# Row maxima of two attention streams transposed and sent in two halves, and a new rule for the order of each engine's work

## The reference, cut to what matters

```python
x = x + tanh(g_xattn[0]) * L0_xattn(layernorm(x), ctx)   # 8 heads of 64, keys from ctx
x = x + tanh(g_ffn[0])   * L0_ffn(layernorm(x))          # 16 heads of 8, self-attention, plus top-2 of 8 experts
x = x + tanh(g_xattn[1]) * L1_xattn(layernorm(x), ctx)   # 16 heads of 8, keys from ctx
x = x + tanh(g_ffn[1])   * L1_ffn(layernorm(x))          # top-2 of 8 experts
```

## Time and profile before

| | |
|---|---|
| Median of 3 runs | 752.5 us (751.01 to 752.66) |
| Profiled execution | 746.59 us |
| Its span, first to last instruction | 744.8 us |
| Mean granted clock of PE in it | 0.933 of full speed |
| Busy in the span | PE 663.1, DVE 569.7, ACT 374.2, POOL 344.5 us |

### The profile page before, as it was taken

One profiled execution on the slowest core, in us unless ns is written; L12 is line 12 of the kernel. 1 busy time (PEld: TensorE's weight loads), 2 busy tenths in 40 slices (PEclk: granted clock), 3 DMA queues, 4 the chain that ended last, 5 costly groups with the idle time before them and its releaser, 6 DMA issues.

```text
span 744.8 us, 13302 instructions
## 1 busy us (share of the span) xinstructions
PE 663.1 (89%) x5232; PEld 336.2 (45%) x5232; DVE 569.7 (76%) x1055; ACT 374.2 (50%) x482; POOL 344.5 (46%) x467
## 2 busy tenths in 40 slices
PE   6699898998999899989999999989999789787684
PEld 2265454553544455434645355534653424333342
DVE  2626578589998879788898979887888987928534
ACT  4064345545546753775357644765357346263360
POOL 4273753852463257415663368326764324422233
PEclk9599999999999999989999999999999969969597
DMA  7210202112101221121121311121013221021000
GB/s 193 80 58 19 86 1 62 45 44 63 43 24 41 77 64 52 52 79 32 41 66 42 99 48 65 36 75 50 22 58 97 71 68 68 4 89 55 7 1 14
DMA packets 45790, 40.82 MB, mean 55 GB/s; under 512 B 4824, under 2 KB 37536, under 8 KB 45728
## 3 DMA queue, kind: packets, MB, share of 16 engines
q1 hardware_dynamic: 45168, 39.52, 17.1%
q10 hardware_dynamic: 560, 0.46, 0.2%
HBM read 22.93 MB, written 17.04 MB: 54 GB/s over the span
## 4 chain that ended last, share of the span: by engine, by line
PE 66%; DVE 21%; ACT 6%; issue 2%; POOL 2%; DMA 2%; SPq 1%; POOLq 0%; DVEq 0%
PE psum L670 13%; PE psum L626 7%; PE psum L590 7%; DVE mx8B L925 7%; PE psum L582 6%; DVE mxA L831 4%; PE psum L658 4%; ACT probB L740 4%; PE psum L557 3%; PE psum L639 3%; PE psum L551 3%; PE psum L600 2%; PE psum L577 2%; DVE rden L839 2%; PE psum L675 2%
## 5 line engine op out<-in xcount | busy, mean ns | idle before, releaser
L925 DVE TENSOR_REDUCE mx8B<-psum 128x2 f32<-128x1024 f32 x128 | 153.7, 1219 | 22.7 <-PE psum L639 21.5
L740 ACT ACTIVATE probB<-psum 128x1024 f32<-128x1024 f32 x128 | 126.4, 1029 | 57.2 <-PE psum L658 56.5
L727 ACT ACTIVATE probX<-psum 128x1024 f32<-128x1024 f32 x64 | 65.5, 1024 | 95.1 <-PE psum L582 94.8
L920 DVE TENSOR_REDUCE mx8F<-psum 128x4 f32<-128x1024 f32 x64 | 77.0, 1217 | 8.8 <-PE psum L633 8.6
L831 DVE TENSOR_REDUCE mxA<-psum 128x2 f32<-128x1024 f32 x64 | 76.6, 1216 | 8.5 <-PE psum L564 8.1
L839 DVE RECIPROCAL rden<-psum 128x256 f32<-128x256 f32 x32 | 56.1, 1752 | 34.8 <-PE psum L594 34.7
L740 ACT ACTIVATE probF<-psum 128x1024 f32<-128x1024 f32 x64 | 65.1, 1026 | 24.0 <-PE psum L658 22.2
L999 POOL TENSOR_TENSOR prodC<-prodC 128x256 f32<-128x256 f32 x30 | 21.8, 725 | 104.6 <-DVE prodC L913 102.3
L670 PE MATMUL psum<-probB,v8B 128*32 128x256 f32 x1024 | 67.5, 408 | 2.8 <-ACT probB L740 2.7
L582 PE MATMUL psum<-qX,kX 64*128 64x256 f32 x512 | 68.4, 388 | 0.0
L991 POOL TENSOR_TENSOR psum_k<-probX 128x512 f32<-128x512 f32 x32 | 40.8, 1274 | 59.5 <-ACT probX L727 58.5
(11 more groups left out here) (192 smaller groups left out, 1174.2 us busy)
## 6 DMA issues: line engine op xcount, KB each, us to landing
k8B<-k_dK SPq DMA_DIRECT2D x32, 192.0 KB
k_dK<-partsK SPq DMA_DIRECT2D x8, 384.0 KB, 2.5
q8F<-q_dF SPq DMA_DIRECT2D x32, 96.0 KB
k8F<-k_dF SPq DMA_DIRECT2D x32, 96.0 KB
q8B<-q_dB SPq DMA_DIRECT2D x32, 96.0 KB
k_dK<-partsK SPq DMA_DIRECT2D x8, 256.0 KB, 2.7
cTX<-in_ctxT SPq DMA_DIRECT2D x8, 192.0 KB, 2.8
cTK<-in_ctxT SPq DMA_DIRECT2D x8, 192.0 KB, 2.4
```

The costliest lines, as they stand in the source:

```text
L727: nc.scalar.activation(prob[s][(8 * b + k) % SLOTS[s]][:], ps, ACT.Exp, scale=float(XD) ** -0.5).then_inc(done["ACT"], 1)
L740: nc.scalar.activation(prob[s][(units * b + k) % SLOTS[s]][:], ps, ACT.Exp, scale=float(D8) ** -0.5).then_inc(done["ACT"], 1)
L920: nc.vector.tensor_reduce(mx8[s][:].rearrange("p t (i q) -> p i t q", i=2)[:, :, :, k], ps.rearrange("p (i t n) -> p i t n", i=2, t=QT), A ...
L925: nc.vector.tensor_reduce(mx8[s][:, t, :].rearrange("p (i q) -> p i q", i=2)[:, :, p], ps.rearrange("p (i n) -> p i n", i=2), AX.X, ALU.ma ...
```

## The change

The maxima of F and B are transposed, sent and read back in two halves of four pairs each. `mT8`, `mw` and `mr` now exist with k = 0 and 1: half 0 needs only the first half of `mx8`, and the first half of `e8` needs only half 0's `mr`. For this the maxima are laid out by half in `mx8`, `m2` becomes 8 rows by 2 halves, and `mw` and `mr` have a semaphore for each half. Each transposition works on 8 columns in place of 16; the two DVE instructions behind it keep their length of 256.

The order changes too. To the longest way of each step an amount is added for its stream and name (`URGENT`) and one for its stream and batch (`TURN`). On PE and DVE the steps whose start lies within 0.05 or 0.1 us of that engine's earliest start now count as equal (`NEAR`), and the greatest sum goes first. `LEAD`, which bounds how far ahead PE may fill for DVE, goes from 2.0 to 1.6, and some planned costs are altered. Every engine's list may come out anew.

The diff, with context lines left out:

```diff
 
-HOP, OUT, LEAD = .07, .18, 2.0
+HOP, OUT, LEAD = .07, .18, 1.6
+
+URGENT = {
+    "X": {"ctx": -1109, "e": -172, "kp": -398, "ln": 216, "ls": 1008, "mT": 1342, "mx": 477, "out": -814, "pv": -153, "qp": 137, "rs": -55, "vp": -490, "xb": -1195, "xh": 530, "xin": 252},
+    "F": {"e8": 21, "fin": -2102, "gate": -183, "gx": 487, "ln": 743, "ls": 1151, "mT8": 231, "moe": -64, "mr": 1131, "mw": -1069, "mx8": 193, "oT": 771, "pv8": -105, "qk": 73, "rs": -745, "sp": -59, "sr": -1648, "sw": 169, "v8": -231, "wT": -347, "wb": 325, "xh": 938},
+    "K": {"ctx": -327, "kk": -1014, "sp": 1076, "sr": -13, "sw": 100, "vv": 455},
+    "B": {"aT": 645, "e8": 1380, "ln": -212, "ls": 322, "mT8": 1441, "mr": -676, "mw": 1051, "mx8": -199, "oT": 200, "out8": 632, "pv8": -884, "qk": 870, "rs": 1173, "sp": 1101, "sr": 1115, "sw": 2256, "xb": 131, "xh": -395},
+    "C": {"fin": -355, "gate": 829, "gx": -964, "ln": 95, "ls": 209, "moe": -468, "out": 474, "rs": -317, "xh": 245},
+}
+TURN = {"X": (-11, 223, -187, 128, -186, -418, -177, -378), "F": (364, 245, -96, -55, -170, 361, -227, -214), "K": (129, 247, -28, -143, 235, -281, -105, 984), "B": (187, -73, 225, 16, -28, 29, -15, 45), "C": (-463, -87, -33, -78, -367, 717, -506, 102)}
+NEAR = {"PE": 0.05, "DVE": 0.1}
 LAND = {"xin": 2.1, "ctx": 2.5, "sw": 2.5, "mw": 1.5, "mr": 2.0, "out": 1.8, "sr": 3.5}
...
     for k in range(maxima):
-        p.fill("DVE", 1, s, "mx8", b, k, .3, 1.22, [("SP", x, "sr", b, 2 * k // maxima) for x in stacked], [("DVE", s, "mT8", b - 1, 0)])
-    p.fill("DVE", 0, s, "mT8", b, 0, .26, .85, [("DVE", s, "mx8", b, maxima - 1)], [("SP", s, "mw", b - 1, 0)])
-    p.job("SP", s, "mw", b, 0, .35, ("DVE", s, "mT8", b, 0), ("SP", s, "mr", b - 1, 0))
-    p.job("SP", s, "mr", b, 0, 1.25, ("SP", s, "mw", b, 0), ("PE", s, "e8", b - 1, units - 1))
+        p.fill("DVE", 1, s, "mx8", b, k, .3, 1.22, [("SP", x, "sr", b, 2 * k // maxima) for x in stacked], [("DVE", s, "mT8", b - 1, 2 * k // maxima)])
+    for k in range(2):
+        p.fill("DVE", 0, s, "mT8", b, k, .26, .85, [("DVE", s, "mx8", b, maxima // 2 * (k + 1) - 1)], [("SP", s, "mw", b - 1, k)])
+        p.job("SP", s, "mw", b, k, .4, ("DVE", s, "mT8", b, k), ("SP", s, "mr", b - 1, k))
+        p.job("SP", s, "mr", b, k, .8, ("SP", s, "mw", b, k), ("PE", s, "e8", b - 1, units // 2 * (k + 1) - 1))
     for k in range(units):
         g = units * b + k - SLOTS[s]
-        p.fill("ACT", 1, s, "e8", b, k, .32, 1.03, [("SP", s, "mr", b, 0)], [("PE", s, "pv8", g // units, g % units // n)])
+        p.fill("ACT", 1, s, "e8", b, k, .32, 1.03, [("SP", s, "mr", b, 2 * k // units)], [("PE", s, "pv8", g // units, g % units // n)])
     for k in range(4):
...
     plan_gate(p, "F", b, (1.2, .95))
-    plan_stack(p, "F", b, 3.9, 6, ("ACT", "F", "qk", b, 0), ("F", "e8"))
+    plan_stack(p, "F", b, 3.1, 6, ("ACT", "F", "qk", b, 0), ("F", "e8"))
     p.fill("DVE", 0, "F", "v8", b, 0, .62, .43, [("ACT", "F", "ln", b, 0)], [("PE", "F", "pv8", b - 1, 3)])
...
     p.fill("ACT", 0, "K", "kk", b, 0, 1.0, 1.4, [("SP", "K", "ctx", b, 0)], [("SP", "K", "sw", b - 1, 0)])
-    plan_stack(p, "K", b, 3.9, 3, ("ACT", "K", "kk", b, 0), ("B", "e8"))
+    plan_stack(p, "K", b, 3.05, 3, ("ACT", "K", "kk", b, 0), ("B", "e8"))
     for k in range(2):
...
     p.fill("DVE", 0, "B", "qk", b, 0, .5, 1.0, [("ACT", "B", "ln", b, 0)], [("SP", "B", "sw", b - 1, 0)])
-    plan_stack(p, "B", b, 2.2, 3, ("DVE", "B", "qk", b, 0), ("B", "e8"))
+    plan_stack(p, "B", b, 1.95, 3, ("DVE", "B", "qk", b, 0), ("B", "e8"))
     plan_attend(p, "B", b, "KB", ("DVE", "K", "vv", b, 1), 2 * NPAIR,
...
     way, later = longest_ways(jobs)
+    way = {key: us + URGENT.get(key[1], {}).get(key[2], 0) + TURN.get(key[1], (0,) * BATCH)[key[3]] for key, us in way.items()}
     left = {key: len(after) for key, (_, after) in jobs.items()}
...
         for e, keys in could.items():
+            found = []
             for key in keys:
...
                         start = max(start, free["DVE"] + line - LEAD - jobs[key][0])
-                rank = start, -way[key]
-                if best is None or rank < best[0]:
-                    best = rank, key, banks
+                found.append((start, -way[key], key, banks))
+            if not found:
+                continue
+            if e in NEAR:
+                soon = min(one[0] for one in found) + NEAR[e]
+                one = min((one for one in found if one[0] <= soon), key=lambda one: (one[1], one[0]))
+            else:
+                one = min(found, key=lambda one: one[:2])
+            if best is None or one[:2] < best[0]:
+                best = one[:2], one[2], one[3]
         (start, _), key, banks = best
...
     "X": dict(xin=16, ctx=16, mv=1, rstd=1, xh=1, xb=1, psum=8, pch=XH, vch=XH // 2 + 1),
-    "F": dict(mv=1, rstd=1, xh=1, split=1, sw=6 * 16, sr0=4 * 16, sr1=4 * 16, lg=1, eg=1, w=1, used=4, fin=1, mw=16, mr=32,
-              xm=2, pch=8, vch=14),
+    "F": dict(mv=1, rstd=1, xh=1, split=1, sw=6 * 16, sr0=4 * 16, sr1=4 * 16, lg=1, eg=1, w=1, used=4, fin=1, mw0=16, mw1=16, mr0=32, mr1=32,
+              xm=2, pch=8, vch=15),
     "K": dict(ctx=16, split=1, sw=3 * 16, sr0=2 * 16, sr1=2 * 16, vch=2),
-    "B": dict(mv=1, rstd=1, xh=1, xb=1, split=1, sw=3 * 16, sr0=2 * 16, sr1=2 * 16, mw=16, mr=32, pch=1, vch=6),
+    "B": dict(mv=1, rstd=1, xh=1, xb=1, split=1, sw=3 * 16, sr0=2 * 16, sr1=2 * 16, mw0=16, mw1=16, mr0=32, mr1=32, pch=1, vch=7),
     "C": dict(mv=1, rstd=1, xh=1, lg=1, eg=1, w=1, used=4, fin=2, out=16, out1=16, pch=8, vch=15),
...
         mx8 = per("FB", "mx8", [P, QT, H8])
-        m2 = per("FB", "m2", [H8, 2, SEQ], BF16)
+        m2 = per("FB", "m2", [NPAIR, 2, 2, SEQ], BF16)
         oU = per("FB", "oU", [P, 4, SEQ])
...
         k_d = {"F": dram("k_dF", [6, P, SEQ], BF16), "K": dram("k_dK", [6, P, KV], BF16)}
-        m2_d = {s: dram("m2_d" + s, [2, H8, SEQ], BF16) for s in "FB"}
+        m2_d = {s: dram("m2_d" + s, [2, 2, NPAIR, SEQ], BF16) for s in "FB"}
 
...
                 elif name == "mw":
-                    sp.wait_ge(*is_done(s, "mT8", b))
-                    sp.wait_ge(*after(s, "mr", b - 1))
-                    engine.dma_start(m2_d[s].rearrange("t h n -> h t n"), m2[s][:]).then_inc(S[s]["mw"], 16)
+                    sp.wait_ge(*is_done(s, "mT8", b, k))
+                    sp.wait_ge(*after(s, f"mr{k}", b - 1))
+                    engine.dma_start(m2_d[s][k].rearrange("t h n -> h t n"), m2[s][:, k, :, :]).then_inc(S[s][f"mw{k}"], 16)
                 elif name == "mr":
-                    sp.wait_ge(*after(s, "mw", b))
-                    sp.wait_ge(*is_full(s, "e8", b - 1, NPAIR * KEYS[s] // SEQ - 1))
+                    sp.wait_ge(*after(s, f"mw{k}", b))
+                    sp.wait_ge(*is_full(s, "e8", b - 1, NPAIR * KEYS[s] // SEQ // 2 * (k + 1) - 1))
                     for i in range(2):
-                        engine.dma_start(q8[s][64 * i + KROWS:64 * i + MROWS],
-                                         m2_d[s].rearrange("t (i p) n -> i t p n", i=2)[i]).then_inc(S[s]["mr"], 16)
+                        engine.dma_start(q8[s][64 * i + KROWS:64 * i + MROWS, 4 * k:4 * k + 4, :],
+                                         m2_d[s][k][:, 4 * i:4 * i + 4, :]).then_inc(S[s][f"mr{k}"], 16)
                 elif name == "out":
...
                 elif name == "mT8":
-                    pe.wait_ge(*is_done(s, "mx8", b, NPAIR * KEYS[s] // SEQ - 1))
-                    for t in range(QT):
-                        last = transpose(ps[0:H8, t * P:(t + 1) * P], mx8[s][:, t, :], ident[:])
+                    pe.wait_ge(*is_done(s, "mx8", b, NPAIR * KEYS[s] // SEQ // 2 * (k + 1) - 1))
+                    for t in range(QT):
+                        last = transpose(ps[0:NPAIR, t * P:(t + 1) * P], mx8[s][:, t, NPAIR * k:NPAIR * (k + 1)], ident[:])
                 elif name == "wT":
...
                 elif name == "e8":
-                    pe.wait_ge(*after(s, "mr", b))
                     p, c0 = (k, 0) if s == "F" else (k // 2, 2 * (k % 2))
+                    pe.wait_ge(*after(s, f"mr{2 * p // NPAIR}", b))
                     for c in range(2):
...
                 elif name == "mx8":
-                    dve.wait_ge(*is_full(s, "mT8", b - 1))
-                    if s == "F":
-                        nc.vector.tensor_reduce(mx8[s][:].rearrange("p t (i q) -> p i t q", i=2)[:, :, :, k],
-                                                ps.rearrange("p (i t n) -> p i t n", i=2, t=QT), AX.X, ALU.max,
-                                                negate=True).then_inc(drained, 1)
-                    else:
-                        p, t = divmod(k, QT)
-                        nc.vector.tensor_reduce(mx8[s][:, t, :].rearrange("p (i q) -> p i q", i=2)[:, :, p], ps.rearrange("p (i n) -> p i n", i=2), AX.X, ALU.max,
-                                                negate=True).then_inc(drained, 1)
+                    n = NPAIR * KEYS[s] // SEQ
```

(11 more changed lines are left out.)

## The result

The changed kernel takes 755.5 us (median of 20 runs, 752.46 to 763.61), the one before 754.25 us over 20 runs beside it (750.38 to 757.58). The ratio is 1.0051, with an interval of 1.0028 to 1.0074: 0.5% slower, 3.8 us. I had forecast 731 us, between 712 and 753, and given a slower kernel 0.17. It is outside the range and on the other side. A few executions ran far longer than their neighbours (781.69 and 787.24 us in the first kernel of experiment 6 and in that of experiment 4, 1236.89 us in that of experiment 5); the ratios leave them out, and the medians given for experiments 4 and 5 are of the others.

The account below looks back on a forecast made before the run. PE was taken to bound 40 to 640 us, a chain of waits the tail. 746.6 - 7.5 - 6 + 6 - 14 = 725.1, plus 5.9 from profiled execution to median: 731 us, range 712 to 753.

Parts of the forecast that it names:

- Part 4: Engine order: fills a quarter of 54 us of PE idle time (40 to 640 us and tail), gaining 14 us.
- part 3: Added transposes, DVE pairs, sends and returns of the halves: +6 us (PE 3.5, DVE 2.5, transfers 0), bounds 0 to 20.
- part 2: Batch 6 of B: half its exponents run earlier, and K comes earlier for batch 7; gain 6 us.
- Part 1: Batch 7 of B: first half's exponents start before the last maxima end; gain 7.5 us, between 3.5 and 9.5.
- (c): Inner batches: PE takes B's exponents back to back, bare stretches lower the clock; three give 766 us, six 783; chance 17%.
- Rival (a): Halves pay, order gives nothing in the full part: median 749 us, 746 with 3 us of order; chance 22%.
- Rival (b): Second half's trip ends last everywhere, added work eats the rest: median 752 us; chance 6%.
- My own tests: m2B sends about 9 us apart, ACT idle about 10, X past 556, PE idle below 31.8, PE busy up at most 7.
- the mark at which I would have called myself wrong: Windows between 100 and 600 us showing PE under 94% busy with clocks under 0.97.

Follow-up runs that it names:

- experiment 6: Changed kernel, planner told of the loads at the start: first kernel keeps the amounts, 741.3 us (0.9863); second has amounts set anew, 736.0 us (0.9754).
- experiment 4: Changed kernel with the start order of before, first halves' DVE copy and subtract cut to 2 columns in batches 1 to 6: 746.3 us (0.9901).
- experiment 5: Changed kernel with batch 7's first eight exponents and two sums of B held until both halves are back: 767.0 us (1.0233).
- experiment 2: Changed kernel's halves under the old order rule: 800.2 us (1.0624); kernel before with the new order rule and whole maxima: 843.1 us (1.1197).

## Why the prediction was wrong

- **Part 4, the order, is the step that failed.** I took a quarter of 54 us of PE's idle time, 14 us. From 752.5 to 731 I had forecast 21.5 us of gain, and the change costs 3.8, a miss of 25 us. 10.5 of them are the late start, shown by taking it away and by adding it to the kernel before. For the rest there is only a subtraction, and experiment 2 shows that the parts don't stand alone. If the halves of batch 7 are worth 8.9 us (the path) to 13.7 (experiment 5), the order and the added work make +12.7 to +17.5 us together; less the late start, +2 to +7, where I had -8 (6 of part 3 less 14). With part 3 between 0 and my 6, the rest of the order gave something between +7 and -4, not -14 (more than that, if part 2 gained anything). At the 20 that part 3 costs in before's order, it would have given -13 to -18; against that price speaks only experiment 4, for the third of DVE's work that it took out. So the late start, for which part 4 had no term, is shown and is less than half of the miss; how the rest divides between part 4 and part 3 stays open. I had written "No rows show the new order" and filled the gap with a share of idle time. Two of the things I leaned on came true and proved nothing: X ends at 596.9 in place of 556.2, but B was not further on for it. B's last maximum of batch 5 ends at about 624 us, in the second trace of before at about 602. And the tail's idle time did fall. The share of idle time in a window that is 94% busy is no measure of what an order can give, and a planner's order is only as good as the constraints it knows: here the weights' loads were not among them. I had costed the order as a whole and never asked which step the amounts would put first, or what that step waits for (`w_loaded`, in the code of PE's loop). My windows began at 40 us. Told of the loads, the same amounts make a kernel of 741.3 us, and new ones 736.0, which would lie in my range.
- **Part 1, batch 7:** right in mechanism, mis-sized. I took 7.5 us, with 9.5 as the bound. On the path from the last maximum to the last exponent it is 8.9, and undoing it costs 13.7, give or take 4. Why more, if it is more, is argued: the tail has other work, fitted around the halves, that then waits too.
- **Part 2, batch 6:** 6 us were taken for K being earlier. No run takes this part alone, so it stays open.
- **Part 3, what the halves add:** +6, "bounds 0 to 20". Done in before's order it is 20, the upper bound, and the split is not mine: I priced PE at 3.5 and it is 6; DVE at 2.5 and it is 17.6; transfers at 0 and they are 1 (-1.4 to 3.5). In the changed order cutting a third of DVE's work showed no gain. So "hidden by PE where PE is the bound" is false of before's order and not refuted in the changed one, and the term has no value apart from an order.
- **Rivals.** (c), the slower one, named the order as the culprit, but by bare stretches of exponents in inner batches. There the middle lost nothing (-2.5 us of idle time, clock 0.97): right in sign, wrong in place. Rival (a), "the halves pay and the order gives nothing", is nearest to the kernel once its start is mended: 745.1 us measured, 746 to 749 forecast. Rival (b), 752, is nearest to the changed kernel itself, but by luck: batch 7 gained what (b) said it would not.
- **The range** ended at 753, below the medians of both kernels: I had added 5.9 us for the difference of the profiled execution to the median of three runs, and over 20 runs the difference is 7.7. A fast execution of before as the base of the sum made every case some 2 us too low.
- **My own tests.** m2B is sent twice, 15.8 us apart and not 9; ACT's stretch is 5.9 and not 10; X ends later than 556; PE idle after 640 is 25.4, under 31.8; PE's busy time is 6.1 above the first trace, under 7. From 100 to 640 PE is busy 94.5% at 0.97, above the mark at which I would have called myself wrong. Every sign that I had named for success came, most of them with another number, and the kernel is slower: none of them looked at the first 40 us.

## What to carry to other kernels

A view of the start (what the first instruction of each engine waits for) belongs to every change of an order: here it is where loads that the planner does not know of decided. An order and the steps it was fitted to are one change, and neither half of it can be priced or tested alone; here they cost 47 and 90 us apart and 4 together. And 13 us more on the engine that is 76% busy cost 18 in one order, where the engines hand PSUM banks to one another; in another, cutting 4.5 us of the same work gained nothing that could be told. Such a term is bounded by an experiment in place and not by which engine "is the bound".

## What the runs showed of the hardware

- Two traces of one program differ by 8.3 us of 750, and 8.1 of them are PE's busy time at the same matmuls and the same idle time (81.7 and 81.9 us), with the granted clock 0.933 and 0.919. A ledger between two kernels is safe in idle time; in busy time it needs several executions of each, or it books the clock of one execution as the change.
- Much more idle time of PE came with a lower clock for the work between it: at 81.9 us idle PE was busy 671.2 us (0.919), at 102.9 us 694.6 (0.895), at 149.3 us 694.1 (0.893). The three kernels with a wait of 18 us ahead of the first matmul break the row: the changed kernel (85.0 us idle, 669.1 busy, 0.936), the one that held batch 7 back (95.5, 669.6, 0.934) and the kernel before with the late start (95.9, 670.4, 0.928). So it matters where the idle time lies. From 30 to 40 us the kernel before is granted 0.50, with the late start 1.00, and the changed kernel 0.66.
- The clock recorded ahead of and in the first work says little. The four matmuls of L551 that begin at 4.61 us take 3.78 us, the same four at 10.92 take 1.88, and the recorded clock is 1.00 over both and over the 18 us of idle time in the changed kernel. By their length the first four ran at the lower of the two levels (1.2 and 2.4 GHz).

```profile
4.00:8.00 4.00, 3.40 (x4) 1.51 (x5) 2.47 (x7) 0.00 (x0) 2.08 (x6) 1.00 0.60 169
8.00:12.00 4.00, 4.00 (x10) 1.80 (x9) 0.00 (x0) 3.13 (x5) 4.00 (x4) 1.00 0.61 172
```

- DVE's copy from PSUM takes 0.41 us over 256 columns with 8 partitions (mean 407 ns) as with 16 (411 ns in the kernel with DVE doubled), so cutting the rows in two saves nothing on it.
